# An RWKV and mixture-of-experts layer on one core: residual rows stored to the output early, and added to by the last scatter

## The reference, cut to what matters

```python
x = L0_attn_x                                   # (8, 2048, 256) float32: 16384 tokens of 256
x = x + layernorm(rwkv_attention(layernorm(x)))
h = layernorm(x)
logits = h @ router_w                           # 8 experts, the 2 best for each token
routed = sum over the 2 of  weight * (silu(h @ w1[e]) @ w2[e])
shared = sigmoid(h @ shared_gate_w) * ((silu(gate) * up) @ shared_down)
out = x + layernorm(routed + shared)
```

## Time and profile before

| | us |
|---|---|
| median of 3 timed runs | 1598.68 |
| their range | 1597.98 to 1603.28 |
| the profiled execution, its own time | 1603.3 |
| its span, first to last instruction | 1601.5 |
| PE busy in the span | 1513.8 |
| DVE busy | 1377.2 |
| ACT busy | 1336.3 |
| POOL busy | 1079.9 |

### The profile page before, as it was taken

The page is one execution under the profiler, slowest core; times in us unless marked ns, Lnnn a source line. Parts: engine busy times, 40 slices in busy tenths (PEclk is TensorE's granted clock), DMA queues, the critical chain, the costliest instruction groups (busy, mean ns, idle before and its releaser), DMA issues.

```text
span 1601.5 us, 35130 instructions
## 1 busy us (share of the span) xinstructions
PE 1513.8 (95%) x9960; PEld 1360.9 (85%) x9960; DVE 1377.2 (86%) x3140; ACT 1336.3 (83%) x2768; POOL 1079.9 (67%) x1168
## 2 busy tenths in 40 slices
PE   5899999999999999999999999689999998999992
PEld 4778888888888888888888888578999998999992
DVE  5899998999999999999999888856877777999993
ACT  5688998899889988999898888756777777999993
POOL 1256677767776766677677766766666664888886
PEclk9999999999999999999999999889999999999996
DMA  4114333533322222222222222138777764777771
GB/s 125 41 55 132 118 113 115 171 106 126 108 95 82 83 85 91 79 86 87 88 82 82 91 72 73 65 100 283 238 238 244 247 207 136 229 223 229 235 239 55
DMA packets 124619, 214.41 MB, mean 134 GB/s; under 512 B 19975, under 2 KB 67338, under 8 KB 124432
## 3 DMA queue, kind: packets, MB, share of 16 engines
q1 hardware_dynamic: 92368, 126.13, 26.1%
q0 software_dynamic: 32064, 86.04, 14.6%
HBM read 116.37 MB, written 99.39 MB: 135 GB/s over the span
## 4 chain that ended last, share of the span: by engine, by line
PE 62%; DVE 12%; issue 10%; POOL 9%; ACT 1%; DMA 1%; DVEq 1%; POOLq 0%; SPq 0%; ACTq 0%
PE PS L1474 53%; POOL d_ys L592 8%; PE PS L1466 3%; PE PS L1538 2%; PE PS L1536 2%; PE PS L1692 2%; DVE rkl L1446 1%; DVE shl L1446 1%; PE PS L1708 1%; DVE x L1405 1%; DVE ysh L1413 1%; DVE dl L1405 1%; DVE xin L1413 1%; POOL out L610 1%; DVE tr L1405 1%
## 5 line engine op out<-in xcount | busy, mean ns | idle before, releaser
L551 POOL DMA_INDIRECT d_xd<-h2n,ixs x248 | 310.3, 1251 | 193.2 <-DVE h2n L1193 127.0
L1474 PE MATMUL PS<-hTh,wqh 128*128 128x512 f32 x768 | 305.1, 397 | 12.3 <-DVE hTl L1114 10.3
L1474 PE MATMUL PS<-hTl,wqh 128*128 128x512 f32 x768 | 305.0, 397 | 0.0
L1474 PE MATMUL PS<-hTh,wql 128*128 128x512 f32 x768 | 305.0, 397 | 0.0
L1474 PEld LDWEIGHTS PS<-hTh,wqh 128*128 128x128 f32 x768 | 145.9, 190 | 46.4 <-issue 10.9
L1474 PEld LDWEIGHTS PS<-hTh,wql 128*128 128x128 f32 x768 | 145.4, 189 | 34.2
L1474 PEld LDWEIGHTS PS<-hTl,wqh 128*128 128x128 f32 x768 | 145.7, 190 | 33.2
L558 POOL DMA_INDIRECT d_xs<-ysh,ixs x124 | 130.6, 1054 | 45.8 <-issue 45.8
L1708 PE MATMUL PS<-weh,h2h 128*128 x380 | 106.4, 280 | 0.0
L1708 PE MATMUL PS<-weh,h2l 128*128 x380 | 106.3, 280 | 0.0
L1708 PE MATMUL PS<-wel,h2h 128*128 x380 | 106.1, 279 | 0.0
(11 more groups left out here) (330 smaller groups left out, 5665.8 us busy)
## 6 DMA issues: line engine op xcount, KB each, us to landing
xin<-in_L_attn_x SPq DMA_DIRECT2D x32, 512.0 KB, 4.3
x<-in_L_attn_x SPq DMA_DIRECT2D x32, 512.0 KB
wqh<-d_xd SPq DMA_DIRECT2D x60, 272.0 KB, 3.5
wql<-d_xd SPq DMA_DIRECT2D x60, 272.0 KB, 2.9
d_xd<-zt SPq DMA_DIRECT2D x18, 272.0 KB
wel<-in_L_ffn_w SPq DMA_DIRECT2D x16, 256.0 KB, 5.1
d_xd<-h2n,ixs POOLq DMA_INDIRECT x248, 2.6
kk<-d_xs SPq DMA_DIRECT2D x12, 256.0 KB
```

Source lines behind the costliest of these rows:

```text
L551: g.indirect_dma_start(d_xd[s], bass.IndirectOffsetOnAxis(ap=ixs[:, m % 2, k:k + 1], axis=0), h2n_of(m)[:, j, :], None).then_inc(s_sct[s], 16)
L1474: ins = mm_(out_ap, l, r, start=(k == 0), stop=(k == len(todo) - 1))
```

## The change

The residual rows `x1` of each chunk are stored to the output by SP in the first stage (one plain DMA of 512 KB a chunk). The last scatter then carries only the normed rows, and adds them to what the output holds (`compute_op=ALU.add`). With that, `back`, `back_second`, the ring `xk` and the `ext` words go. `final` becomes a multiplication by one per-row factor. The step from sums of squares to variances moves from POOL to DVE (`last_variance`). The loads of 272-word rows stay as they were.

```diff
 SP, first stage, step i
+                if on(i - 4):
+                    sp.wait_ge(s_x1, n(i - 4, NT, NT))
+                    sp.dma_start(out_v[i - 4], x1[:, :, :]).then_inc(s_xo, 16)
                 if 0 < i - 3 < NCH:
                     sp.wait_ge(s_h2, n(i - 3 - 1, NT, NT))
+                    sp.wait_ge(s_xo, 16 * (i - 3))
                     sp.dma_start(x1[:, :, :], x_v[i - 3]).then_inc(s_xr, 16)
...
+            sp.wait_ge(s_xo, 16 * NCH)
 POOL, first stage
-            g.memset(ext[:, :, :, :], 0.0).then_inc(s_const, 1)
+            g.memset(h2n[:, :, C_EXT:XW], 0.0).then_inc(s_const, 1)
...
-                g.tensor_tensor(ext[:, m % 2, :, 0], var[:, 2, :], rstd[:, 2, :], ALU.mult).then_inc(s_ex, 1)
-                g.tensor_scalar(ext[:, m % 2, :, 1], nmx[:, m % 4, :], -1.0, None, ALU.mult).then_inc(s_ex, 1)
...
-                    pool.wait_ge(s_ex, n(m, 2, 2))
-                    g.tensor_copy(h2n_of(m)[:, :, C_EXT:XW], ext[:, m % 2, :, :]).then_inc(s_exc, 1)
-                    pool.wait_ge(s_exc, m + 1)
+                    if m == NCH - 1:
+                        g.memset(h2n_of(m)[:, :, C_EXT:XW], 0.0).then_inc(s_exz, 1)
+                        pool.wait_ge(s_exz, 1)
 POOL, second 71 blocks
-                pool.wait_ge(s_sqw, 2 * (2 * q + many))
+                pool.wait_ge(s_vaw, q + 1)
...
-                g.tensor_scalar(varw[:, q % NPR, at], sqw[:, q % NPR, at], 1.0 / D, EPS, ALU.mult, ALU.add).then_inc(s_vaw, 1)
-                pool.wait_ge(s_vaw, q + 1)
...
+                if v == 0:
+                    pool.wait_ge(s_xo, 16 * NCH)
                 pool.wait_ge(s_fin, 2 * (v + 1))
                 for j in range(2):
                     g.indirect_dma_start(out_r, rows_at(w, j, C_TOK), yb[w % NYB][:, j, :], None,
-                                         bounds_check=N - 1, oob_is_err=False).then_inc(s_yo[w % NYB], 16)
+                                         bounds_check=N - 1, oob_is_err=False, compute_op=ALU.add).then_inc(s_yo[w % NYB], 16)
 ACT, second 71 blocks
-                A.activation(xk[v % 4][:, 1, :], xb[w % NX][:, 1, 0:D], ACT.Identity, bias=..., scale=...).then_inc(s_backa, 1)
 DVE, second 71 blocks
-                V.tensor_scalar(xk[v % 4][:, 0, :], xb[w % NX][:, 0, 0:D], ..., ALU.mult, ALU.add).then_inc(s_back, 1)
+            def last_variance(q):
+                many = min(2, NB1 - 2 * q)
+                at = slice(0, 2 * many)
+                dve.wait_ge(s_sqw, 2 * (2 * q + many))
+                if q >= NPR:
+                    dve.wait_ge(s_rsw, q - NPR + 1)
+                V.tensor_scalar(varw[:, q % NPR, at], sqw[:, q % NPR, at], 1.0 / D, EPS, ALU.mult, ALU.add).then_inc(s_vaw, 1)
...
-                    V.scalar_tensor_tensor(out=t, in0=t, scalar=rsw[...], in1=xk[v % 4][:, j, :], op0=ALU.mult, op1=ALU.add).then_inc(s_fin, 1)
+                    V.tensor_scalar(t, t, rsw[...], None, ALU.mult).then_inc(s_fin, 1)
...
             for t in range(NB + 6):
+                v = t - 6 - NB1
+                if v >= 0 and v % 2 == 0:
+                    last_variance(v // 2)
```

More of the change, by code:

```diff
@@ L57, in rwkv_moe @@
     x_v = x.rearrange("b (c j p) d -> (b c) p j d", j=NT, p=P)
+    out_v = out.rearrange("b (c j p) d -> (b c) p j d", j=NT, p=P)
     out_r = out.rearrange("b t d -> (b t) d")
@@ L147, in rwkv_moe @@
         tok = sb("tok", [P, NT])
-        ext = sb("ext", [P, 2, NT, NEXT])
         sqw = sb("sqw", [P, NPR, 4])
@@ L227, in rwkv_moe @@
         s_nb = [sem(f"s_nb{n}") for n in range(3)]
-        s_ex = sem("s_ex")
-        s_exc = sem("s_exc")
+        s_exz = sem("s_exz")
+        s_xo = sem("s_xo")
         s_nx = sem("s_nx")
@@ L308, in rwkv_moe @@
         s_rsw = sem("s_rsw")
-        s_back = sem("s_back")
-        s_backa = sem("s_backa")
         s_fin = sem("s_fin")
@@ L340, in rwkv_moe @@
         assert len(xb) == NX and len(yb) == NYB
-        xk = [flat(t)[:, i * 2 * D:(i + 1) * 2 * D].rearrange("p (j d) -> p j d", j=2) for t in (ysh, xin) for i in range(2)]
         xTh = [hTh[:, 0, 0:TC], rkh[:, 0, :]]
@@ L515, in scale_in @@
                     pool.wait_ge(s_nb[2], c - 3)
-                    pool.wait_ge(s_ex, n(c - 4, 2, 2))
                 norm_scale(0, c, mv[:, 0, :, :], nmx[:, c % 4, :])
@@ L535, in scale_h2 @@
                 g.tensor_tensor(nb[:, 2, :], nmx[:, m % 4, :], rstd[:, 2, :], ALU.mult).then_inc(s_nb[2], 1)
-                if m >= 2:
-                    pool.wait_ge(s_exc, m - 1)
-                g.tensor_tensor(ext[:, m % 2, :, 0], var[:, 2, :], rstd[:, 2, :], ALU.mult).then_inc(s_ex, 1)
-                g.tensor_scalar(ext[:, m % 2, :, 1], nmx[:, m % 4, :], -1.0, None, ALU.mult).then_inc(s_ex, 1)
             def scatter(m, s):
@@ L924, in last_squares @@
                                  accum_out=sqw[:, q % NPR, 2 * k + j:2 * k + j + 1]).then_inc(s_sqw, 1)
[L926 to L932, removed]
             for t in range(NB + 4):
@@ L955, in _ @@
                     last_squares(t - 4 - NB1)
-                    back_second(t - 4 - NB1)
         @block.vector
@@ L1418, in final @@
                 dve.wait_ge(s_rsw, q + 1)
-                dve.wait_ge(s_back, v + 1)
-                dve.wait_ge(s_backa, v + 1)
                 for j in range(2):
                     t = yb[w % NYB][:, j, :]
-                    V.scalar_tensor_tensor(out=t, in0=t, scalar=rsw[:, q % NPR, 2 * k + j:2 * k + j + 1],
-                                           in1=xk[v % 4][:, j, :], op0=ALU.mult, op1=ALU.add).then_inc(s_fin, 1)
+                    V.tensor_scalar(t, t, rsw[:, q % NPR, 2 * k + j:2 * k + j + 1], None, ALU.mult).then_inc(s_fin, 1)
             for t in range(NB + 6):
+                v = t - 6 - NB1
+                if v >= 0 and v % 2 == 0:
+                    last_variance(v // 2)
                 if t == 9:
@@ L1454, in _ @@
                     y_out(t - 3)
-                if 0 <= t - 3 - NB1 < NB1:
-                    back(t - 3 - NB1)
                 if t - 6 >= NB1:
```

## The result

The change takes 1661.7 us in the median (1659.1 to 1663.8), the kernel before 1598.9 beside it. The ratio is 1.0368, with a 95% interval of 1.0342 to 1.0395: 62.8 us more. I had forecast 1590, and 1632 as the upper end of the range.

The account below looks back on a forecast made before the run. POOL, DVE and ACT were taken to bound the second 71 blocks at 3.44 us each, POOL then at 3.30: 9.9 us less, 1.0 more for the last landing, 1598.7 - 8.9 = 1590; range 1582 to 1632.

Parts of the forecast that it names:

- I take nothing: POOL, second 71 blocks: an adding scatter's issue costs 0 more; bounds nothing to 0.97 us for each of 142.
- The rival's own formula: Longer adding-scatter issue on POOL: x us more each puts 142x on the end; break-even 0.063 us; chance 0.25.
- my upper bound of 1.42: DMA engines, second 71 blocks: each added row counted as three, 1.42 us more a block; 0.71 was taken.
- that rival: DMA engines become the bound in the second 71 blocks, from 0.86 us more a block; 1639 us at 4.0; chance 0.09.
- the sum: Second 71 blocks: 35.5 pairs x 0.28 = 9.9 us less, 1.0 more for the last landing, so 8.9 less.
- the root's wait for DVE's variances: POOL, second 71 blocks: its root now waits for variances made at the start of the DVE step; no cost counted.
- Relieving only one of the three would give nothing: Second 71 blocks: POOL, DVE and ACT all stand at 3.44 us a block, so relieving one gains nothing.
- The port rival: Second 71 blocks: DVE's new multiplications hold up POOL's scatters, 3.48 us a block, +3 us, 1602; chance 0.08.
- the room on DVE and ACT: Second 71 blocks: DVE falls from 3.44 to 2.92 us a block, ACT to about 2.94, leaving holes.
- The landing: The last adding scatter's landing at the kernel's end: now 3.6 us, 0 to 3.6 more, 1.0 taken.
- a longer issue at L610's successor: Sign that the forecast is wrong: a longer issue of the output scatter on POOL.
- nothing comes of it: Second 71 blocks: a loop through the three engines holds 3.44 us a block and stays, 1598 us; chance 0.11.

Follow-up runs that it names:

- run 2: The changed kernel with the adding scatter's bound at row 0, so every row but one is skipped: 1657.9 us, ratio 1.0350.
- run 1: The changed kernel without the addition, its last scatter a plain one that overwrites: 1595.6 us, ratio 0.9959 to the kernel before.
- run 9: The changed kernel with only 64 rows listed in each output scatter, added: 1651.1 us in one execution, beside 1602.2.
- run 10: The changed kernel with only 64 rows listed in each output scatter, overwriting instead of adding: 1590.3 us in one execution, beside 1602.2.
- run 3: The changed kernel without POOL's reciprocal root, rows scaled by the variance, adding scatters kept: 1627.8 us, ratio 1.0162 to the kernel before.
- run 5: The changed kernel with half as many adding scatters, rows twice as long, into a table of its own: 1603.7 us, ratio 1.0008.
- run 12: The changed kernel without the addition and with variances made by ACT's squares instead of DVE: 1590.0 us, ratio 0.9917 to the kernel before.
- run 8: The kernel before with only the variances of a pair moved from POOL to DVE: 1611.2 us, ratio 1.0055.
- run 11: The kernel before without POOL's variance step, folded into ACT's squares by a scale and a bias: 1611.5 us, ratio 1.0051.
- run 4: The kernel before with only the first-stage store of the residual rows and its waits added: 1603.4 against 1603.2 us, ratio 1.0000.
- run 7: The changed kernel with overwriting scatters; SP loads 256 rows a block and DVE's `final` adds them: 1612.8 us, ratio 1.0062.

## Why the prediction was wrong

**The step that failed: the issue of the adding scatter on POOL, "I take nothing".** Two kinds of plain issue were compared there, with all rows and with most rows skipped, and both cost about 1 us. From that I concluded that the length "hardly follows the rows that it moves", which is right: run 2 shows it for the addition too. But it says nothing of what an addition costs, and I used it as if it did. The issue pays for the kind of DMA and for the rows listed: 1543 against 982 ns for 128 rows (runs 1 and 2), 1418 against 910 for 64 (runs 9 and 10). That is +0.56 in the undisturbed case, and +0.35 to +0.53 beside the four issues of the earlier trace rows, taken in order; those sum to 4.37, the new ones to 1.59 + 3 x 1.55 = 6.24, so 0.47 each. The rival's own formula then gives -8.9 + 142 x 0.47 = +58. By the mean over all 142 issues, 1.596 us against 1.093, it gives +62.5, where +62.8 was measured. The formula, its break-even at 0.063 us and its place were right; its chance of 0.25 was too low, and the range ended at a price of 0.29 us, though the bound written down was 0.97.

**DMA time: mis-sized.** I took 0.71 us a block for the plain scatters, from the whole queue, and 0.71 more for the addition. From 1340 on the output scatters have POOL's queue to themselves. The DMA view from there to 1601 for the kernel before, then to 1662 for the change:

```profile
DMA packets 25112, 51.52 MB, mean 197 GB/s; under 512 B 4752, under 2 KB 4753, under 8 KB 25070
...
q0 software_dynamic: 6816, 16.79, 17.2%
```

```profile
DMA packets 38918, 51.86 MB, mean 161 GB/s; under 512 B 6119, under 2 KB 22503, under 8 KB 38877
...
q0 software_dynamic: 20448, 16.80, 43.2%
```

17.2% of 261 us are 44.9, which is 0.63 a block; 43.2% of 322 us are 139.1, or 1.96. The addition costs 1.33 us more a block, close to my upper bound of 1.42 and past the 0.86 from which that rival decides. Rows that are skipped cost little: 3.4% of 316 us in run 2, 0.15 a block. So an added row of 1 KB took the engines 3.1 times a plain one. The packets differ too: with the addition 22503 - 6119 = 16384 are between 512 B and 2 KB, one for each token's row, and before only one was; there 6816 packets held all the rows, several to a packet. The Trainium skill, Collectives: The Full Stack, section "The bandwidth ceiling: the fold count and why AG ≠ RS ≠ AR", gives a reduction over a ring half the rate of a copy, for its two source reads. By that an added row would cost twice a plain one; the measurement decides. POOL hid this: at 0.88 x 4.27 = 3.76 us of DMA time a block, an estimate from the changed kernel's own rows, the engines would not have let the stage run at 3.30 had the issue been free. Runs 3 and 5 show PE waiting for loads as soon as POOL is relieved.

**The gain, without the addition.** Run 12 has the pair of 6.60 us that the sum was made of (6.58), and is 13 us faster than before. From its first scatter to its last are 1576.2 - 1345.3 = 230.9 us, where the kernel before took 240.7: 9.8 less, which is the sum's 9.9. The mechanism was right. The rest lies ahead of the first scatter, which comes 6.0 us earlier in that execution; the prediction put nothing there, and no run explains it. Run 1 got only 7.6 us. The prediction named the root's wait for DVE's variances and priced it at nothing; run 1's roots wait, and run 12, without that wait, is faster.

**"Relieving only one of the three would give nothing."** Not tested. Runs 8 and 11 were meant to relieve POOL alone, but run 8 gives DVE the instruction, and run 11 makes ACT's squares longer. Both lose about 0.5%, and in run 11 a pair grows by just what ACT got. That fits three engines with the same pace and no slack. The 0.05 to 0.23 us by which DVE seemed to stretch POOL's issues are no constant: in run 8 the same four scatters take more in every other pair. Which instruction of DVE's does it stays open. The port rival's own form falls: with the two new multiplications in place run 1's issues were 982 ns in the median of its group, against 1116 before.

**Right as written:** the store (run 4), the first stage and the first 71 blocks, and the room on DVE and ACT. The landing came out smaller than the 1.0 us taken: 4.1 us against 3.6. The list of signs named the deciding one, "a longer issue at L610's successor". Of the rivals, "nothing comes of it" fell with runs 1 and 12.

## What to carry to other kernels

A DMA with an operation in it is another instruction than the plain one, on the engine that issues it and on the DMA engines: price it by a run of its own before building on it, above all where the issuing engine has no slack. A constant length over cases of one kind is no evidence for another kind. Where several engines run at the same pace without slack, work that is taken from one and put on another made the whole slower, so relieve them together. And look at the trace before calling a run's change one-sided: an operand added to an instruction can lengthen it.

## What the runs showed of the hardware

- An adding scatter of 128 rows took POOL 1.54 us to issue, a plain one 0.98. The rows skipped cost the issue as much as those moved (run 2). Rows of 2 KB took no longer at the shortest, 1.54 us (run 5).
- The adding scatters of 1 KB rows kept the 16 DMA engines busy 1.96 us a block of 256 rows, plain ones 0.63. Each added row was a packet of its own; plain rows shared packets.
- PE waited 18.6 us for loads in run 7, at a DMA share of 0.88, and 6.2 in run 1, at 0.72.
- Two instruction lists on POOL and DVE that run beside each other moved POOL's issues between 0.97 and 1.53 us, with the same DMAs in them (run 8).
- A square of 128x256 with its sum took ACT 406 ns, and 500 with a scale and a bias tile (run 11).
